# Softplus of the scan layers by way of |x| on ScalarE, in place of a clamp and a maximum on VectorE

## The reference

```
xz = einsum('bld,ed->ble', x, in_w);  xi, z = split(xz, 2)
xc = silu(conv1d(xi, cw) + cb)                    # 256 channels, 4 taps
dt, Bm, Cm = split(einsum('bld,ed->ble', xc, xp_w), [8, 24])
delta = softplus(einsum('blr,dr->bld', dt, dtw) + dtb)
A = -exp(A_log)                                   # 256 channels x 16 states
# for each t:  h = exp(delta_t * A) * h + delta_t * xc_t * B_t ;  y_t = sum over states of h * C_t
y = (y + xc * D) * silu(z)
x = einsum('bld,od->blo', y, ow)
```

## Time and profile before

| | us |
|---|---|
| median of 3 runs | 1147.46 |
| lowest and highest | 1146.35, 1148.29 |
| the profiled execution | 1143.46 |
| its span on the core | 1141.7 |
| scan stage in it (to the end of the last `out`) | about 770 |

### The profile page before, as it was taken

How to read it: one execution, slowest core, us unless ns; L and a number is a source line. 1 busy time by engine, 2 the same in 40 slices (tenths; PEclk the granted TensorE clock), 3 DMA queues, 4 the chain that set the end, 5 groups by cost and what they waited for, 6 DMA issues and landing times. The chain is left out here.

```text
span 1141.7 us, 25505 instructions
## 1 busy us (share of the span) xinstructions
PE 970.5 (85%) x9849; PEld 514.2 (45%) x9849; DVE 948.4 (83%) x1737; ACT 769.8 (67%) x1690; POOL 774.8 (68%) x425
## 2 busy tenths in 40 slices
PE   5799999999999999999999998871774999998375
PEld 2344444444434444444444444431453666675254
DVE  3599999999999999999999999969891456664995
ACT  4888889889898888897988878813331245544332
POOL 1488988989989889889898898963341123322252
PEclk9999999999999999999999999985786599998788
DMA  6554444435443436353445443307201011000001
GB/s 241 175 181 132 150 133 149 149 105 199 128 150 131 149 115 197 121 168 125 139 140 158 123 159 115 130 1 158 31 1 19 1 20 20 13 9 2 0 1 38
DMA packets 65420, 119.17 MB, mean 104 GB/s; under 512 B 40004, under 2 KB 46980, under 8 KB 56324
## 3 DMA queue, kind: packets, MB, share of 16 engines
q1 hardware_dynamic: 65300, 117.54, 33.1%
HBM read 109.13 MB, written 6.29 MB: 101 GB/s over the span
## 5 line engine op out<-in xcount | busy, mean ns | idle before, releaser
L845 POOL TENSOR_TENSOR prod<-hid,c_rep 128x1024 f32<-128x1024 f32 x256 | 612.8, 2428 | 97.0 <-DVE hid L778 96.9
L778 DVE TENSOR_TENSOR_SCAN hid<-decay,acc 128x256 f32<-128x256 f32 x1024 | 609.9, 664 | 37.4 <-PE acc L498 33.9
L682 ACT ACTIVATE decay<-delta,a_neg 128x255 f32<-128x255 f32 x1024 | 428.0, 497 | 60.6 <-DVE hid L778 60.2
L498 PE MATMUL acc<-b_diag,du_t 64*64 64x256 f32 x4096 | 273.9, 383 | 35.5 <-DVE hid L778 35.5
L521 PE MATMUL ring<-prod,ident 64*64 64x512 f32 x2048 | 245.2, 594 | 4.4 <-POOL prod L845 3.8
L498 PEld LDWEIGHTS acc<-b_diag,du_t 64*64 64x64 f32 x4096 | 145.9, 133 | 199.5 <-issue 114.5
L1661 POOL TENSOR_SCALAR_AFFINE_SELECT att_probs<-att_probs 128x512 f32<-128x512 f32 x64 | 40.6, 634 | 133.2 <-ACT att_probs L1705 133.2
L521 PEld LDWEIGHTS ring<-prod,ident 64*64 64x64 f32 x2048 | 78.2, 134 | 103.2 <-issue 82.2
L1705 ACT ACTIVATE att_probs<-acc 128x384 f32<-128x384 f32 x128 | 55.8, 488 | 78.9 <-PE acc L1472 78.9
L413 PE MATMUL ring<-xpad,diag_cw 64*64 64x512 f32 x512 | 60.5, 589 | 1.0 <-ACT xpad L606 0.9
L1470 PE MATMUL acc<-att_qk 17*128 17x256 f32 x256 | 56.6, 460 | 0.5 <-ACT att_probs L1705 0.4
(11 more groups left out here) (166 smaller groups left out, 1349.5 us busy)
## 6 DMA issues: line engine op xcount, KB each, us to landing
c_rep<-c_rows SPq DMA_DIRECT2D x64, 1024.0 KB, 4.8
b_diag<-diag_rows SPq DMA_DIRECT2D x64, 512.0 KB, 3.8
diag_rows<-prod SPq DMA_DIRECT2D x2, 2048.0 KB, 10.6
att_qk<-in_pos_q SPq DMA_DIRECT2D x4, 768.0 KB
att_qk<-att_dense SPq DMA_DIRECT2D x32, 64.0 KB
att_qk<-in_pos_k SPq DMA_DIRECT2D x4, 288.0 KB
resid<-in_x SPq DMA_DIRECT2D x4, 256.0 KB, 3.1
c_rows<-bc SPq DMA_DIRECT2D x64, 8.0 KB, 1.5
```

Source lines behind the costliest of these rows:

```text
L498: last = nc.tensor.matmul(inj[m * HALF:(m + 1) * HALF, K % 2, at:at + HALF * SG], du_t[rows, n % 2, e, chans:chans + HALF], b_diag[rows, K ...
L682: last = nc.scalar.activation(decay[:, K % DECAYS, s, 1:], delta[:, n % 2, h, e * SEQ + 1:(e + 1) * SEQ], ACT.Exp, scale=a_neg[:, lay(n) % ...
L778: last = nc.vector.tensor_tensor_scan(hid[:, K % HIDS, s, :], decay[:, K % DECAYS, s, :], rows[:, s, :], 0.0, ALU.mult, ALU.add)
L845: nc.gpsimd.tensor_tensor(prod[:, K // 4 % 2, h, :, at], hid[:, K % HIDS, :, :], c_rep[:, g, :, at], ALU.mult).then_inc(s_prod, 1)
```

## The change

The clamp on VectorE goes. ScalarE forms |delta| (new function `magnitude`, at k = 5), then exp(-|delta|) and, at k = 6, ln(1 + .). VectorE's second step stays where it is and becomes one instruction that computes max(delta, 0) + soft. The semaphore `s_clamp` is replaced by `s_abs`. In the first pair the steps are done ahead of the loop in the same order.

```diff
-                def softplus(n):
-                    a.wait_ge(s_clamp, n + 1)
-                    nc.scalar.activation(soft[:, :, :], soft[:, :, :], ACT.Exp).then_inc(s_exp, 1)
+                def magnitude(n):
+                    ring.wait_read(a, "dt1", n)
+                    need(a, s_delta, n)
+                    nc.scalar.activation(soft[:, :, :], delta[:, n % 2], ACT.Abs).then_inc(s_abs, 1)
+
+                def softplus_exp(n):
+                    a.wait_ge(s_abs, n + 1)
+                    nc.scalar.activation(soft[:, :, :], soft[:, :, :], ACT.Exp, scale=-1.0).then_inc(s_exp, 1)
+
+                def softplus_log(n):
                     a.wait_ge(s_exp, n + 1)
                     nc.scalar.activation(soft[:, :, :], soft[:, :, :], ACT.Ln, bias=core.one[:, :]).then_inc(s_log, 1)
...
+                            if k == 5:
+                                magnitude(n + 1)
+                                softplus_exp(n + 1)
                             if k == 6:
-                                softplus(n + 1)
+                                softplus_log(n + 1)
...
-                def clamp(n):
-                    ring.wait_read(v, "dt1", n)
-                    need(v, s_delta, n)
-                    nc.vector.tensor_scalar(soft[:, :, :], delta[:, n % 2], EXP_MAX, None, ALU.min).then_inc(s_clamp, 1)
-
                 def softplus(n):
                     v.wait_ge(s_log, n + 1)
-                    nc.vector.tensor_tensor(delta[:, n % 2], delta[:, n % 2], soft[:, :, :], ALU.max).then_inc(s_delta, 1)
+                    nc.vector.scalar_tensor_tensor(delta[:, n % 2], delta[:, n % 2], 0.0, soft[:, :, :], ALU.max, ALU.add).then_inc(s_delta, 1)
...
                         if n + 1 < NPAIR:
-                            if k == 5:
-                                clamp(n + 1)
                             if k == 7:
                                 softplus(n + 1)
```

More of the change, by code:

```diff
@@ L253, in mamba_stage @@
         s_crep = [sem(f"c{g}_spread") for g in range(SG)]
-        s_gate, s_exp, s_log = sem("gate_ready"), sem("softplus_exp"), sem("softplus_log")
-        s_clamp, s_delta, s_du = sem("clamped"), sem("delta_ready"), sem("du_ready")
+        s_gate, s_abs, s_exp, s_log = sem("gate_ready"), sem("softplus_magnitude"), sem("softplus_exp"), sem("softplus_log")
+        s_delta, s_du = sem("delta_ready"), sem("du_ready")
         s_zero, s_rows0, s_diag_rows = sem("diagonals_zeroed"), sem("diagonal_rows_zeroed"), sem("diagonal_rows_stored")
@@ L700, in _ @@
                 first_copy(2)
-                softplus(0)
+                magnitude(0)
+                softplus_exp(0)
+                softplus_log(0)
                 read_bt(0)
@@ L803, in _ @@
                     first_norm(p)
-                clamp(0)
                 softplus(0)
```

## The result

| | us |
|---|---|
| changed kernel, median of 4 runs | 1173.55 (1170.24 to 1177.90) |
| kernel before, median of 4 runs | 1147.05 (1146.35 to 1148.29) |
| ratio, 95% interval | 1.0239, 1.0212 to 1.0267 |
| profiled execution after, and its span | 1170.24, 1168.5 |
| forecast | 1174.5, range 1160 to 1181 |

What follows compares the result with a forecast made beforehand. The prediction took a loop through TensorE's and ScalarE's legs, closed by `b_t`, as the bound. ScalarE's lengthened leg less GpSimd's wait, +14.2, and clock falls, +12.9, gave +27.1 us on 1147.5: 1174.5 us, range 1160 to 1181.

Steps and rivals of the forecast that it cites:

- The loop of two legs: Scan stage: TensorE's 32.60 us and ScalarE's 11.82 us with their hand-overs make the whole 44.76 us period of a pair.
- The clamp's value of 0: VectorE: removing the clamp frees 3.03 us per pair, none of it on the path that sets the period.
- The Abs: ScalarE's leg: the added |delta| lengthens it by 0.97 us per pair, 16 times, 15.5 us.
- Max and add: VectorE's second softplus step: 1.28 us, bounds 1.1 and 2.6, value 0 either way.
- GpSimd: Next layer's diagonals: the 1.06 us wait of VectorE for GpSimd should vanish, 3 x 0.43 = −1.3 us.
- The clock: TensorE: one 3.1 us wait ahead of out makes its clock fall in 13 of 15 pairs, +12.9 us.
- The share that I had thought would be lost in waiting: TensorE: half speed beginning during the wait partly costs nothing, so 1.5 us was taken per fall.
- the same two waits: TensorE at 153 us: waits of 1.57 and 0.72 us, then slow out; said to happen in 4 of 14 pairs.
- The rival without more falls: TensorE's clock: no more falls, ScalarE's term alone, +14.2, 1161 us; with a few more falls 1163 to 1167; 22%.
- Busy times: Scan stage: VectorE's busy time down by up to 40 us, ScalarE's up by about 16 us.
- the sum: Whole kernel: 14.2 + 12.9 = +27.1 us over the kernel before.
- ScalarE's term: ScalarE's leg: 16 x 0.97 = 15.5 us for the Abs, less 1.3 us for GpSimd, +14.2 us.

Runs made afterwards that it cites:

- experiment 1: Kernel before without the clamp, exp reading delta itself and nothing added: 1148.72 us, ratio to before 1.0003.
- experiment 5: Kernel before without the clamp, TensorE's injection of sub 8 made twice over: 1139.23 us, ratio to before 0.9943.
- experiment 6: Kernel before with the clamp, TensorE's injection of sub 8 made twice over: 1139.45 us, ratio to before 0.9947.
- the better order: Kernel before, clamp kept: ScalarE reads bt, then exp and ln, ahead of k = 6's decays; reads out at start of k = 7: 1135.49 us.
- the other two: Same ScalarE order as the better order: changed kernel 1121.93 us; kernel with neither clamp nor Abs 1120.48 us.
- experiment 8: Kernel before, clamp kept, ScalarE's read of bt moved to start of k = 6 and of out to start of k = 7: 1184.92 us.
- experiment 3: Changed kernel with TensorE's injection of sub 8 made three times over: 1152.36 us, ratio to before 1.0038.
- experiment 2: Kernel before, clamp and maximum kept, plus an Abs per pair on ScalarE into an unread tile: 1169.22 us, ratio to before 1.0192.
- experiment 4: Changed kernel with ScalarE's read of bt moved from k = 7 to the start of k = 6: 1135.47 us, ratio to before 0.9886.
- experiment 10: Changed kernel, read of bt and ln ahead of k = 6's decays, read of out at start of k = 7: 1121.93 us, ratio to before 0.9798.
- experiment 7: Changed kernel, ScalarE's read of bt moved to start of k = 6 and of out to start of k = 7: 1122.64 us, ratio to before 0.9787.

## Why the prediction was right

The forecast was +27.1 us between profiled executions; it was 1170.24 − 1143.46 = 26.8. Step by step:

- **The bound.** The loop of two legs was right: the wait for `b_t` is there, longer, and experiments 1, 5 and 6 show that VectorE, at 95%, is not the bound.
- **The clamp's value of 0** was right in the kernel as it stands (1148.72 against 1149.06 us). It holds only as long as the wait for `b_t` stands behind it; in the better order the kernel with the clamp is 13.6 us and more slower than the other two, and a part of that at least is the clamp's.
- **The Abs** was forecast at 1.06 us of work and 0.97 us of period. It took 1.05, and the period without a fall grew from 44.75 to 45.68 us, 0.93.
- **Max and add** was put at 1.28 us and took 1.52. It cost nothing, as said. The reason for the length is below.
- **GpSimd.** The 1.06 us waits at the layers' second pairs (one of 0.8 us is left in the loop) and the periods of 45.19 us are gone; the pair 298.06 to 343.74 is one of them, at 45.68. That is the 1.3 us, as forecast.
- **The clock** was right in kind and mis-sized in its two factors, in opposite senses: 13 of 15 waits at 1.5 us were forecast, 11 of 14 at 1.64 us were found, so 18.0 us in place of 19.5. The share that I had thought would be lost in waiting was not there. Two readings behind the forecast number of falls were off, and both make its closeness partly luck. The prediction speaks of "the same two waits" at the present falls; but three of the four stand behind 1.57 and 0.72 us, which occur only three times, and one behind 1.19 and 1.00 us, which occur eleven times. And the wait of 2.35 us in the last pair, read as one that leaves the clock at full, was followed by 1.2 GHz in 7 of the 13 profiles of this study. (The rival without more falls counts 11 pairs of 14 at full clock; it is 10.)
- **Busy times.** VectorE's fell by 30.7 us (up to 40 forecast) and ScalarE's rose by 14.5 (16 forecast).
- **What had not been forecast.** The stages behind the scans, in which nothing changed, took 2.7 us more in this profile: 1168.5 − 793.7 = 374.8 us from the last `out` on, against 1141.7 − 769.6 = 372.1. Over the 13 profiles of this study it is 372.1 or 372.2 three times (the kernel before and experiments 6 and 8) and 374.8 to 375.1 ten times, whatever the kernel. Inside the scan stage the change was +24.1 us, 3 us under the sum. So part of the closeness of the total is luck.

The rival without falls, 1161 us, is what experiment 3 shows: 1152.4 us when the present falls are gone too, which is 13 us over the 1139.5 us of experiment 6, the kernel before likewise filled. ScalarE's term was forecast as 14.2. Here too luck has a part: in the two profiles the scan stage ends 10.4 us apart (775.9 and 765.5 us), and another 2.8 us lie in the stages behind.

## What to carry to other kernels

When several engines are over 85% busy, add up one period from the timelines, leg by leg between the waits, and see whether the legs close; only what lies in a leg counts, and the engine with the highest share need not be in one. A wait is free as long as a second wait behind it on the same engine takes up whatever the first one loses, and it becomes dear when the second one goes: after each repair look for the wait that stands next, in the same queue. A short instruction that releases another engine (here a read of 0.26 us) belongs as far ahead in its queue as its own input allows, and no further, since one that has to wait holds up all that stands behind it.

## What the runs showed of the hardware

**TensorE's clock and waits.** One wait of 3.2 us per pair was followed by 1.2 GHz in 11 of 14 pairs (the changed kernel), one of 2.3 us in 7 of 14 (experiment 1). Of two waits with 1.09 us of work between them, 1.57 and 0.72 us were followed by it in 3 of 3 pairs and 1.19 and 1.00 us in 1 of 11 (the kernel before); 1.18 and 1.96 us, with the same work between them, in 12 of 14 (experiment 2). A single wait of 1.7 us was followed by it in 1 of 12 (experiment 4), single waits of 1.2 to 1.55 us by none (experiments 3, 5 and 6). So the same wait is followed by a fall in one pair and not in the next, and its length alone does not decide; what else does, no run here shows. Matmuls that compute the same thing again, put into the wait, made the changed kernel 21 us faster.

**VectorE and GpSimd exclude each other in some instructions.** VectorE's second step of softplus, with two tensors in SBUF, ends 1.08 to 1.09 us after GpSimd's product in progress, however long before that it started, in every pair of the 11 profiles in which one is in progress: 281.15 against 280.07 in experiment 10, 298.12 against 287.61 + 9.42 = 297.03 in the changed kernel, 256.52 against 255.44 in experiment 8.

```profile
287.61 9.42 POOL L849 TENSOR_TENSOR prod<-hid,c_rep 128x1024 f32<-128x1024 f32 x4 [1.07 <-DVE hid L785]
```

With no product in progress it took 1.22 to 1.23 us (the new form in experiments 4 and 7, the old one in the first pair of the kernel before). GpSimd waits the other way: in the kernel before, the product that starts 0.16 us after the maximum took 3.34 us in each of 15 pairs, all others 2.34 to 2.42. The first of these two took 2.31 us here, so the second 3.34:

```profile
286.81 5.65 POOL L845 TENSOR_TENSOR prod<-hid,c_rep 128x1024 f32<-128x1024 f32 x2 [2.96 <-DVE hid L778]
```

The clamp, which has one tensor, took 2.54 us in the earlier trace rows, though alone it would be far shorter: over all 16 the profile gives

```profile
L766 DVE TENSOR_SCALAR soft<-delta x16: 693/2534/2915, 26.1 to 690.3; 128x1024 f32<-128x1024 f32 x16
```

that is 0.69 us at the least, in the first pair, ahead of any product. In the loop it ends 0.55 us after the product in progress each time. The scans, whose second tensor lies in PSUM, run beside the products: all of them took 0.65 to 0.69 us. So 1.85 of the clamp's 2.54 us, 4 of VectorE's 95 points, was time in which it stood for GpSimd and was shown as busy. The Trainium skill, "VectorE: DVE Perf Modes", section on two Vector instructions with no wait between them, names a second SBUF read interface that is shared with GpSimd and that is used by instructions with two SBUF tensors and by those in a 2-port mode; for the steps with two tensors these rows agree with that, and show the price. That the clamp runs in a 2-port mode would fit its rows, but is not shown.
